# A four-block image network: attention moved to whole float32 on image pairs, its depthwise convolution moved from TensorE to GpSimd

## The reference

```python
# L1_ffn, E = 16 experts: every token goes through all experts, two have a weight above 0
h1, h2 = einsum('bsd,edh->bseh', x, w1), einsum('bsd,edh->bseh', x, w2)
expert_out = einsum('bseh,eho->bseo', silu(h1) * h2, w3)
y = einsum('bseo,bse->bso', expert_out, dispatch)

# L2_conv, 8 heads of 16; HW = 256 pixels of one image
q   = einsum('oc,bchw->bohw', wq, fmap)
kdw = depthwise_3x3(fmap, wdw)                  # padding 1, one 3x3 filter per channel
k, v = split(einsum('oc,bchw->bohw', wpw, kdw), 2)
q = softmax(q over its 16 columns) * 16 ** -0.5 # per token and head
k = softmax(k over the 256 pixels)
out = einsum('bnd,bde->bne', q, einsum('bnd,bne->bde', k, v))
y = einsum('oc,bchw->bohw', wout, gelu(out)) + bout

# L2_ffn, E = 8 experts with their own norm gain ln_g and bias ln_b; top 2
h = gelu((xn * ln_g[e] + ln_b[e]) @ W1[e] + b1[e]);  y_e = h @ W2[e] + b2[e]
```

## Time and profile before

| | us |
|---|---|
| median of 3 runs | 703.14 |
| lowest, highest | 700.75, 706.04 |
| profiled execution, first to last instruction (span) | 693.4 |
| PE busy / DVE / ACT / POOL in it | 613.2 / 439.8 / 363.3 / 257.4 |

### The profile page before, as it was taken

How to read it: one execution, slowest core, us unless ns; L and a number is a source line. 1 busy time by engine, 2 the same in 40 slices (tenths; PEclk the granted TensorE clock), 3 DMA queues, 4 the chain that set the end, 5 groups by cost and what they waited for, 6 DMA issues and landing times.

```text
span 693.4 us, 11977 instructions
## 1 busy us (share of the span) xinstructions
PE 613.2 (88%) x3648; PEld 401.5 (58%) x3648; DVE 439.8 (63%) x1305; ACT 363.3 (52%) x760; POOL 257.4 (37%) x348
## 2 busy tenths in 40 slices
PE   8898785777989999999998898879999999998783
PEld 6685324774545555555556676877545545467652
DVE  6555596888897787787786577565233333336556
ACT  3335686266534444443437554454666766736384
POOL 6402555340544542542464000180233333326163
PEclk9998995598999999999999999967999999999696
DMA  4900000205344252432501000020522222100001
GB/s 111 157 11 1 2 0 1 61 1 121 69 96 95 68 116 61 100 83 61 121 1 39 1 2 1 1 50 2 129 61 61 61 69 82 31 2 1 1 2 61
DMA packets 24531, 34.61 MB, mean 50 GB/s; under 512 B 10984, under 2 KB 20224, under 8 KB 22368
## 3 DMA queue, kind: packets, MB, share of 16 engines
q1 hardware_dynamic: 24480, 33.95, 21.1%
HBM read 32.50 MB, written 1.44 MB: 49 GB/s over the span
## 4 chain that ended last, share of the span: by engine, by line
PE 51%; DVE 12%; issue 3%; ACT 2%; POOL 2%; DVEq 0%; ACTq 0%; POOLq 0%
PE ps L1811 11%; PE ps L2376 10%; PE ps L2392 9%; PE ps L1831 5%; PE ps L2499 2%; PE ps L2808 1%; DVE ST L490 1%; PE ps L1589 1%; PE ps L2104 1%; PE ps L2114 1%; PE ps L2092 1%; POOL out_acc L1500 1%; PE ps L2135 1%; DVE m_between L556 1%; PE ps L2116 1%
## 5 line engine op out<-in xcount | busy, mean ns | idle before, releaser
L1500 POOL TENSOR_TENSOR out_acc<-out_acc,tok_tmp 128x512 f32<-128x512 f32 x80 | 103.3, 1291 | 219.6 <-DVE tok_tmp L1715 118.4
L1811 PE MATMUL ps<-tokT,w 128*128 128x512 f32 x512 | 135.8, 410 | 4.8 <-DVE hid_buf L1710 3.2
L1772 ACT ACTIVATE act_buf<-ps 128x512 f32<-128x512 f32 x128 | 75.8, 597 | 94.8 <-PE ps L1811 89.2
L1811 PEld LDWEIGHTS ps<-tokT,w 128*128 128x128 f32 x512 | 92.0, 190 | 55.9 <-issue 24.3
L2376 PE MATMUL ps<-tokT,w 128*128 128x512 f32 x256 | 69.7, 416 | 0.0
L2376 PEld LDWEIGHTS ps<-tokT,w 128*128 128x128 f32 x256 | 47.3, 195 | 26.6 <-ACT hid_buf L2358 11.4
L1710 DVE TENSOR_TENSOR hid_buf<-act_buf,ps 128x512 f32<-128x512 f32 x64 | 43.3, 685 | 20.1 <-ACT act_buf L1772 14.9
L535 ACT ACTIVATE U<-X,nmr,rstd 128x64 f32<-128x64 f32 x116 | 40.4, 428 | 22.5 <-POOL nmr L513 17.3
L1710 DVE TENSOR_TENSOR tok_split<-act_buf,ps 128x512 f32<-128x512 f32 x64 | 43.2, 685 | 12.6 <-ACT act_buf L1772 12.2
L2358 ACT ACTIVATE hid_buf<-ps,b 128x512 f32<-128x512 f32 x64 | 38.6, 682 | 19.8 <-PE ps L2376 17.0
L2358 ACT ACTIVATE tok_split<-ps,b 128x512 f32<-128x512 f32 x64 | 38.9, 688 | 13.9 <-PE ps L2376 13.7
(11 more groups left out here) (478 smaller groups left out, 1123.1 us busy)
## 6 DMA issues: line engine op xcount, KB each, us to landing
disp_all<-disp_dram SPq DMA_DIRECT2D x32, 512.0 KB, 6.2
disp_all<-disp_dram SPq DMA_DIRECT2D x32, 256.0 KB, 3.9
w_raw<-in_L_ffn_w SPq DMA_DIRECT2D x4, 512.0 KB, 8.8
XIN<-in_x SPq DMA_DIRECT2D x4, 256.0 KB, 4.0
w_raw<-in_L_ffn_W SPq DMA_DIRECT2D x2, 512.0 KB, 5.9
out<-XIN SPq DMA_DIRECT2D x4, 256.0 KB, 2.2
fc_raw<-in_L_conv_upfc_w SPq DMA_DIRECT2D x1, 512.0 KB, 4.8
w<-in_L_ffn_w SPq DMA_DIRECT2D x1, 512.0 KB, 10.6
```

What stands on the lines that cost most here:

```text
L1500: pool.tensor_tensor(out_acc[:, :], out_acc[:, :], weighed[p % 2], ALU.add).then_inc(mm["acc"].sem, 1)
L1772: act.activation(act_buf[e % 2][:, :], ps[:, e % 2, :], ACT.Silu).then_inc(mm["act"].sem, 1)
L1811: last = pe.matmul(ps[:, 2 * k + e % 2, :], w12[:, part, k, EXPERT1[e], :], tokT[:, bass.ts(i, CHUNK)], start=(part == 0), stop=(part == 1))
```

## The change

- **Attention in float32 on image pairs.** The split of tokens, of the query weights and of the filter goes. A group's normalised tokens are transposed as pairs (`d_tr`, four 128x128 transposes per group instead of eight), so that partitions 0 to 63 hold one image and 64 to 127 the other. Queries, keys and values are products of 64 rows, the two halves of the array in turn, for a whole group at a time.
- **Transposes in the experts' loop.** `d_tr` and the copies `d_padded` of groups 0, 1, 2 stand in chunks 3, 5, 7 of `e1`; group 3 follows inside the attention.
- **Depthwise convolution on GpSimd.** Per group 17 instructions over 128x512: nine `tensor_scalar` on a shifted window of the padded images (n = 0 and odd n) and eight adds. They stand in `between`, ahead of `chunk_rstd`, in chunks 3 to 7; half of group 2 and all of group 3 follow behind the last chunk. Each waits for its own end (`plink`).
- **Order.** Keys, queries and values of group 0 move ahead of the end of `e1`; `att(g)` starts as soon as its group is ready; ScalarE's loop over chunks is written out. All `keep_clock` calls in `d` and `e2` go.
- **`bias_tensor`** moves from chunk 0 of `e2` to the end of the attention. **`quantise`** moves from the attention to chunk 0 of `e2` (two steps per pair), the `taps` of the last convolution from chunk 0 to chunk 1, `router_transpose` from behind hidden unit 7 to behind unit 11. The weights it reads have a buffer of their own and are loaded after the attention.

```diff
@@ e1_pool
             def between(i, p):
 
+                for g, n in dw_steps(i, p):
+                    dw_pool(pool, g, n)
                 if i == 0 or (i == 1 and p == 1):
...
                     chunk_rstd(pool, i - 1, eps_c, m["d_var"], m["d_rstd"])
             add_weighed(pool, e1, PAIRS1, between)
             chunk_rstd(pool, NCHUNK - 1, eps_c, m["d_var"], m["d_rstd"])
+            for n in range(9, DW_STEPS):
+                dw_pool(pool, G - 2, n)
+            for n in range(DW_STEPS):
+                dw_pool(pool, G - 1, n)
+        DW_STEPS = 17
+        def dw_steps(i, p):
+            if i < 3:
+                return []
+            if i % 2 == 1:
+                first, count = (0, 2, 3, 4, 6, 7, 8)[p - 1], (2, 1, 1, 2, 1, 1, 1)[p - 1]
+            else:
+                first, count = (9, 11, 12, 13, 15, 16, 17)[p - 1], (2, 1, 1, 2, 1, 1, 0)[p - 1]
+            return [((i - 3) // 2, n) for n in range(first, first + count)]
+        def dw_pool(pool, g, n):
+            t = (n + 1) // 2
+            dy, dx = t // 3, t % 3
+            whole = dw_out[:, g, :]
+            if n % 2 == 0 and n > 0:
+                plink(pool.tensor_tensor(whole, whole, tap_prod[t % 2][:, :], ALU.add))
+                if n == DW_STEPS - 1:
+                    pool.sem_inc(m["d_kd"].sem, 1)
+                return
+            if n == 0:
...
+                pool.wait_ge(*m["d_xp"](g + 1))
+            xp = padded_pair[g % 2][:, :, :].rearrange("p q (y x) -> p q y x", x=PADW)
+            dst = whole if n == 0 else tap_prod[t % 2][:, :]
+            plink(pool.tensor_scalar(dst.rearrange("p (q y x) -> p q y x", q=2, x=W), xp[:, :, dy:dy + H, dx:dx + W],
+                                     dw_raw[:, t:t + 1], 0.0, ALU.mult, ALU.add))
@@ d_vector
+            q_norm(dve, 0)
+            for g in range(1, G):
+                q_center(dve, g)
+                k_max(dve, g)
+                ctx_out(dve, g - 1)
+                q_norm(dve, g)
+            ctx_out(dve, G - 1)
@@ d_scalar
+            k_exp(0)
+            q_exp(0)
+            v_move(0)
+            k_move(0)
+            for g in range(1, G):
+                q_exp(g)
+                if g == 1:
+                    chunk_norm(act, NCHUNK - 1, m["d_rstd"], m["d_u"])
+                v_move(g)
+                k_exp(g)
+                if g == 1:
+                    d_padded(act, G - 1)
+                q_move(g - 1, 0)
+                k_move(g)
+                q_move(g - 1, 1)
+            gelu(0)
+            q_move(G - 1, 0)
...
@@ d_tensor
+            keys(0)
+            e1_outp(pe, NCHUNK - 1, E1 // 4 - 1)
+            q_logits(0)
+            values(0)
+            experts_back(pe, e1, PAIRS1, NCHUNK - 1)
+            k_tr(0)
+            for g in range(1, G):
+                q_logits(g)
+                keys(g)
+                values(g)
+                context(g - 1)
+                if g == 1:
+                    pe.wait_ge(*e1["ta"](NCHUNK + 1))
+                    d_tr(pe, G - 1)
+                q_tr(g - 1, 0)
+                k_tr(g)
+                q_tr(g - 1, 1)
             att(0)
+            context(G - 1)
+            q_tr(G - 1, 0)
+            att(1)
+            proj(0)
+            q_tr(G - 1, 1)
+            att(2)
+            proj(1)
+            att(3)
+            proj(2)
+            proj(3)
+            bias_tensor(pe)
@@ e2_vector, e2_tensor (chunk 0 has prev None)
                     if prev is None:
+                        for step in (2 * p, 2 * p + 1):
+                            quantise(dve, step)
                         continue
...
             chunk(0, None)
-            with vchain.loop(1, NCHUNK, 3) as i:
+            chunk(1, 0, taps=True)
+            with vchain.loop(2, NCHUNK, 3) as i:
...
-                    if p == 1 and prev is None:
-                        bias_tensor(pe)
-                        keep_clock(pe, 5, 4)
                     for u in range(4 * p, 4 * p + 4):
                         hidden(i, u)
+                    if p == 2 and prev is None:
+                        router_transpose(pe, mm, route2, 0, (6,))
                     if p == 1 and prev is None:
-                        router_transpose(pe, mm, route2, 0, (6,))
                         wwait(pe, "e2w2")
-                        taps_tensor(pe, 1)
```

More of the change, by code:

```diff
@@ L1783, in e1_scalar @@
             chunk(1, 0, second=True)
-            with act.Fori(2, NCHUNK) as i:
+            for i in range(2, NCHUNK):
                 chunk(i, i - 1)
@@ new lines, in ctx_out @@
+        def ctx_out(dve, g):
+            dve.wait_ge(*m["d_ke"](g + 1))
+            if g == 0:
+                dve.wait_ge(*m["d_hm"](3))
+            vlink(dve.reciprocal(rks[:, BG * g:BG * g + BG], ksum[:, BG * g:BG * g + BG]))
+            dve.wait_ge(*m["d_c_ps"](g + 1))
+            for n in range(BG):
+                b = BG * g + n
+                last = dve.scalar_tensor_tensor(CTX[:, b, :], ps[:, 6, n * INNER:(n + 1) * INNER], rks[:, b:b + 1],
+                                                hmask[:, :], ALU.mult, ALU.mult)
+            last.then_inc(m["d_c"].sem, 1)
@@ new lines, in d_scalar, with d_tr @@
+            gelu(1)
+            q_move(G - 1, 1)
+            gelu(2)
+            gelu(3)
+            for g in range(2):
+                ln_norm(act, g, e2["rstd"], e2["xu"])
+        ATT_BANK = (2, 0, 2, 0)
+        def d_tr(pe, g):
+            pe.wait_ge(*m["d_u"](2 * g + 2))
+            if 1 <= g < G - 1:
+                pe.wait_ge(*m["d_xp"](g))
+            for i in range(4):
+                last = pe.transpose(ps[:, TR_BANK[g], i * P:(i + 1) * P], pair(U, g * TG + 2 * i), ident[:, :])
+            last.then_inc(m["d_ft_ps"].sem, 1)
@@ new lines, in q_tr, with att @@
+                for i in range(4):
+                    last = pe.transpose(ps[:, 7, i * P:(i + 1) * P], q_buf[g % 2][:, 4 * r + i, :], ident[:, :])
+                last.then_inc(m["d_qt_ps"].sem, 1)
+            def att(g):
+                pe.wait_ge(*m["d_c"](g + 1))
+                pe.wait_ge(*m["d_qt"](2 * g + 2))
+                if g == 0:
+                    pe.wait_ge(*m["d_ql"](G))
+                elif g == 1:
+                    pe.wait_ge(*m["d_kt"](G))
+                else:
+                    pe.wait_ge(*m["d_g"](g - 1))
+                for n in range(BG):
+                    r, q = n // QG, n % QG
+                    at = (BG * g + n) * PIX
+                    last = pe.matmul(ps[:, ATT_BANK[g] + r, q * PIX:(q + 1) * PIX], CTX[:, BG * g + n, :], q_T[:, at:at + PIX],
```

472 lines of the change are left out of this document (180 added, 292 removed).

## The result

The changed kernel takes 690.41 us (median of 8 runs, 685.59 to 693.32) against 700.65 us before (8 runs, 695.38 to 706.05); ratio 0.986, interval 0.9812 to 0.9908. In a second comparison, with ten runs of it and thirteen of the kernel before, the ratio was 0.9894 (0.9845 to 0.9944).

A forecast was written before the change was run, and what follows sets the result against it. TensorE was taken to bound the experts' loops, with its waits ending on GpSimd. First experts +11.9, attention -19 and second experts +8.5 gave +1.4 us: span 694.8, plus 9.7 around it, written as 705 us; range 691 to 718.

The forecast's parts named there:

- the 9.7 us around it: Whole kernel: time assumed outside the profiled span, added to the predicted span of 694.8 us to give 704.5.
- the sum of +1.4: Whole kernel: predicted net change of the span, 11.9 - 19 + 8.5 = +1.4 us.
- A: First experts' loop: GpSimd's convolution steps delay scale and last adds, making TensorE wait; +11.9 us (+8.5 to +17).
- B: Attention: shorter although GpSimd's last group makes TensorE wait; last addition to X 19 us earlier (bounds -24 to -8).
- The last adds: Ends of chunks 3 to 6, first experts: a GpSimd step before the last add delays TensorE's transposes, 3.6 us together.
- The scale: First experts, behind chunks 3 to 6: GpSimd's steps make the scale 1.85 us later each, 7.4 us in all.
- The filter's weights: First experts, chunk 1: no longer laid out there, giving back about 0.5 us.
- C: Second experts: later weights' copy 2.2 us, quantise on VectorE in chunk 0 6.3 us; +8.5 us (+4 to +11).
- GpSimd hides its work: Rival, first experts' loop: GpSimd's steps never delay scale and last add; loop +0.9, sum -9.6 us; chance 0.27.
- Windows are slow: Rival, GpSimd's convolution: a window takes 1.40 us instead of 0.8, adding 9.8 us, time 714.5; chance 0.18.
- the clock stays low: Rival, attention: TensorE runs at the lower clock up to the first projections, +7.9 us, time 712.5; chance 0.13.
- Quantise costs nothing: Rival, second experts: chunk 1 takes up quantise's delay, leaving +2.2 us there, time 698.2; no separate chance.

## Why the prediction was wrong

**The ground of the sum.** The largest miss was no step of the change but the last term of the sum. The prediction added "the 9.7 us around it" to the span. Around a span lie 1.7 us. The other 8.0 were the distance between the profiled execution and the median of the three runs. On its own ground, 695.1 us, the sum of +1.4 would have read 696.5, inside the range, and 6 us above the result instead of 14.6. That mends the number and not the change: between the two profiled executions the time fell by 1.8 us, between the medians by 10.2. The kernel before varies more than the changed one, and the attention is where its two profiles differ most (79.5 and 87.8 us, against 50.6 to 50.8); one execution, and a short one, could not show that. How long the attention was in the runs of the median isn't recorded.

**A, first experts: mechanism right, size too large by 6.0 us.** The forecast is 18.0 us of growth up to the last add (11.9, and 6.1 of late adds booked under B); measured 12.0. Both waits are where they were put, and moving GpSimd's steps away from the two places takes the growth back (203.8). The last adds were sized well: put at 3.6 us for chunks 3 to 6, and TensorE's waits for them are 0.54, 1.27, 0.53 and 1.26 (0.2 in all before). Mis-sized were these terms.
- The scale, 1.85 us later in each chunk and 7.4 in all: from the first of the two adds to it are 4.67 us instead of 3.11, so 1.56 more, and the wait of the normalisation and that of TensorE grew by 1.3 (3.40 - 2.09, 1.61 - 0.30), 5.2 in all. The window took 0.69 us instead of 0.8, and an add ahead of another instruction 1.24 to 1.28 from start to start in two of three cases, instead of 1.37. Chunks of "27 to 28 us" came out at 26.7 and 27.9. Together chunks 3 to 6 grew by 9.8 us, where scale, last add and transposes were put at up to 12.4. (Three times half of 1.09 us is 1.6, not the 1.4 put for the transposes; four take 0.60.)
- The filter's weights, "about 0.5" given back in chunk 1: from the loop's start to the second back transposes, which lie behind these steps, it is 2.6 us less (58.0 to 55.4). Of these, 0.6 are the wait for the last add of chunk 0 (0.95 to 0.31) and 1.0 two waits for VectorE in chunk 1 (0.81 and 0.20) that are gone. No run puts the weights back, so their share isn't shown.
- The last chunk's adds ended 4.9 us later, not 6.1.

The page that the prediction weighed, GPSIMD Engine Reference of the Trainium skill, section 4.1, has one-input operations at about line rate, an estimated 0.43 us here; this case's trace has 0.69 and doesn't agree.

**B, attention: right in its order, too long by 3.6 us.** GpSimd does end last, TensorE waits 5.49 us for it where "about 5" was forecast. From the last add on 54.2 us were put and 50.6 measured. GpSimd's two groups took 34.8 us instead of 35.9. From the last keys to X it was 15.7 us instead of 18.3. The clock did what was feared, 0.51 between 410 and 415 us and 1.00 from there, but the products that it slowed were mis-sized: keys and values took 3.8 us (2.08 and 1.71 from start to start), where 2.85 and 3.5 for the clock were put. A group's values, put at 1.9 us at the upper level, take 1.05 there (at 396.01, clock 1.00). The row behind "thinly used" had TensorE busy for 4.00 of 4.00 us, so it showed the lower level but not that reason for it. One sentence isn't borne out: "All other products removed (convolution, splits) lie inside this chain; where they were was the old bound." By the run without the convolution TensorE would have waited for two thirds of that time anyway (12.8 of 18.2 us). What the old bound was as a whole stays open; no other part of the old attention was tried alone.

**C, second experts: right, and two costs unseen.** Forecast +8.5, 2.2 from the weighing's delay and 6.3 from quantise; measured 1.8 and 5.3. The 1.8 depend on the execution (0.3 and 2.0 in the other two profiles of the changed kernel), the 5.3 don't. Undoing each gives them back (router 2.8 to 4.4, quantise 5.3 with the router early). Unseen were 2.6 us ahead of the second experts, which two of the changed kernel's three profiles show and which go with the bias products at half the clock, and 2.4 us in the chunks behind. The latter go with the clock too: from the first to the second back transposes the three profiles have 16.3, 17.9 and 19.1 us, at a granted clock between 490 and 500 us of 1.00, 0.83 and 0.66. "The gain isn't in the end" was right for the bias products; that they could cost something was not considered.

**The rivals.** "GpSimd hides its work" is false for the order of the change: the loop grew by 12 us. It is nearly true of GpSimd's amount of work: in its gaps the same steps cost 0.6 us in chunks 3 to 6 and 2.7 in the last. "Windows are slow" was excluded by 0.69 us, "the clock stays low" by 15.7 us behind the keys. "Quantise costs nothing" fell with 5.3 us.

In all, up to the first addition to X the sum was 10.3 us above this profile and behind it 7.4 below (part of that differs between profiles of one kernel), and its ground was off by 8.0. The steps that it named were the ones that count; their sizes and the ground put it on the wrong side of the line.

## What to carry to other kernels

An engine that is idle half the time is free only in its gaps: before giving it work, list the instructions on it that another engine waits for, and put nothing ahead of those. Against the loop without them, the same steps cost 15.0 us in one order and 3.3 in the other. And ask what the profiled execution itself took: a sum made against a span must not be compared with a median of other executions, as long as a few microseconds decide.

## What the hardware showed

- One program, two executions of its attention: TensorE's granted clock was 1.00 throughout in the profile that the prediction read (79.5 us, TensorE busy 67.8), and 0.90 in the second (87.8 us, busy 76.0), with the same instructions and with the same waits of 5.8 and 2.6 us at the head of the list.

```profile
363.42:451.18 87.76, 76.02 (x431) 62.27 (x432) 51.97 (x108) 43.33 (x101) 8.35 (x11) 0.90 0.04 8
```

- Fewer products can make TensorE no less busy: with 64 products left out the clock was 0.79, and 367 products took as long as 431.
- A fused multiply-add on VectorE over 256 columns, read in rows of 16 out of a padded image and chained on its own output, took 0.49 us (median of 16), but 1.4 each in the four that ran while GpSimd made adds over 512 columns; GpSimd's window over 512 such columns took 0.69.
- A VectorE instruction over 4 columns took 1.26 us (L553 at 279.02) and ended with GpSimd's add that began at 278.96, where the median of its group is 0.16: it is held, as SBUF — State Buffer of the Trainium skill, section "Who interferes with whom", has it; the trace agrees.
